# Random-feature attention with four heads side by side, one ring of banks, and the first cross-attention queries made a stage earlier

## What is computed

```python
# L0_attn, per head h: q, k, v are 112 x 16; omega is 16 x 64
qf = exp(q @ omega - 0.5 * sum(q*q))       # 112 x 64
kf = exp(k @ omega - 0.5 * sum(k*k))       # 112 x 64
kv  = kf.T @ v                             # 64 x 16, the sums
z   = kf.sum(0)                            # 64
out = (qf @ kv) / (qf @ z + 1e-6)          # numerator / denominator
x = layernorm(x + concat(out) @ Wout + bout)
# L0_xattn: q = x @ Wq + bq, keys and values from the text, softmax over 375
```

## Time and profile before

| | us |
|---|---|
| median of 3 runs (lowest to highest) | 1277.84 (1275.55 to 1280.85) |
| time of the profiled execution | 1264.48 |
| its span, first to last instruction | 1262.6 |
| granted TensorE clock over the span | 0.901 |
| PE busy | 1054.4 (84%) |
| DVE / ACT / POOL busy | 663.6 / 581.2 / 281.5 |

### The profile page before, as it was taken

The page is one execution under the profiler, slowest core; times in us unless marked ns, Lnnn a source line. Parts: engine busy times, 40 slices in busy tenths (PEclk is TensorE's granted clock), DMA queues, the critical chain, the costliest instruction groups (busy, mean ns, idle before and its releaser), DMA issues.

```text
span 1262.6 us, 20956 instructions
## 1 busy us (share of the span) xinstructions
PE 1054.4 (84%) x8288; PEld 758.4 (60%) x8288; DVE 663.6 (53%) x1646; ACT 581.2 (46%) x1368; POOL 281.5 (22%) x285
## 2 busy tenths in 40 slices
PE   7988678888784777788999878888988888778996
PEld 4677446566444777545556566666766666445654
DVE  3322455556673767345445547776676774535103
ACT  5411237545334555344444525555565564455542
POOL 2410213200150000332112110222212222232543
PEclk9876759879886999898999999999999998768998
DMA  9420225410455683354224304431332105000001
GB/s 321 92 44 1 55 64 123 129 28 11 165 175 201 217 324 123 115 164 148 85 71 139 120 33 152 125 99 34 90 98 75 50 1 208 1 1 1 1 1 30
DMA packets 66593, 123.63 MB, mean 98 GB/s; under 512 B 11536, under 2 KB 42224, under 8 KB 62416
## 3 DMA queue, kind: packets, MB, share of 16 engines
q1 hardware_dynamic: 63728, 117.48, 30.4%
q0 software_dynamic: 1536, 3.67, 0.9%
q10 hardware_dynamic: 1232, 1.15, 0.3%
HBM read 86.30 MB, written 35.92 MB: 97 GB/s over the span
## 4 chain that ended last, share of the span: by engine, by line
PE 56%; DVE 19%; ACT 10%; DMA 5%; POOL 4%; SPq 3%; issue 3%; DVEq 0%; ACTq 0%; POOLq 0%
PE psum L385 39%; ACT s_p L2469 2%; DVE s_p L2511 2%; POOL rs L2801 2%; PE psum L1205 2%; DMA values<-s_v 2%; DVE s_max L2500 2%; PE psum L2428 2%; PE psum L2439 2%; PE psum L1177 1%; PE psum L2600 1%; DVE s_pT L2492 1%; SPq L960 1%; DVE s_max L1330 1%; DVE wu L1150 1%
## 5 line engine op out<-in xcount | busy, mean ns | idle before, releaser
L2469 ACT ACTIVATE s_p<-psum,s_max 112x375 f32<-112x375 f32 x128 | 72.3, 569 | 85.9 <-DVE s_max L2500 85.9
L633 POOL TENSOR_TENSOR rstd<-meanvar,minus_half 112x1 f32<-112x1 f32 x40 | 23.3, 584 | 315.1 <-DVE meanvar L608 271.2
L1330 DVE TENSOR_REDUCE s_max<-psum 112x2 f32<-112x750 f32 x64 | 59.4, 935 | 39.3 <-PE psum L1177 38.5
L2801 POOL TENSOR_TENSOR rs<-ms,minus_half 112x32 f32<-112x32 f32 x8 | 43.5, 5442 | 110.2 <-DVE ms L2735 110.2
L385 PE MATMUL psum<-ctx,Wk 128*128 128x375 f16 x320 | 62.3, 330 | 5.0 <-ACT s_yT L2058 2.8
L385 PE MATMUL psum<-Wv,ctx 128*125 128x512 f16 x240 | 59.7, 410 | 8.0 <-issue 2.7
L2500 DVE TENSOR_REDUCE s_max<-psum 112x1 f32<-112x375 f32 x128 | 63.7, 539 | 2.1 <-PE psum L2420 2.1
L2428 PE MATMUL psum<-ident,s_p 112*125 112x112 f32 x384 | 59.6, 288 | 4.7 <-DVE s_p L2511 3.0
L1274 ACT ACTIVATE s_pT<-psum 125x672 f32<-125x672 f32 x64 | 46.7, 731 | 32.2 <-PE psum L1193 30.6
L3111 POOL TENSOR_TENSOR hidden<-raw,hidden 128x448 f16<-128x448 f32 x44 | 45.7, 1038 | 65.3 <-ACT hidden L2994 63.6
L587 ACT ACTIVATE s_v<-psum 125x512 f32<-125x512 f32 x48 | 28.5, 596 | 67.3 <-PE psum L385 47.8
(11 more groups left out here) (353 smaller groups left out, 2570.0 us busy)
## 6 DMA issues: line engine op xcount, KB each, us to landing
keys<-s_k SPq DMA_DIRECT2D x64, 187.5 KB, 2.2
s_k<-keys SPq DMA_DIRECT2D x8, 1500.0 KB, 7.4
values<-s_v SPq DMA_DIRECT2D x48, 224.0 KB
s_v<-values SPq DMA_DIRECT2D x16, 672.0 KB
raw_wg<-in_wg SPq DMA_DIRECT2D x8, 1024.0 KB, 5.8
raw_wu<-in_wu SPq DMA_DIRECT2D x8, 1024.0 KB, 5.7
raw_wd<-in_wd SPq DMA_DIRECT2D x8, 1024.0 KB, 5.3
s_kd<-k_halves SPq DMA_DIRECT2D x48, 93.8 KB, 3.9
```

Of the source, the lines that this page charges most:

```text
L1330: VE.tensor_reduce(s1_max[b % 2][:, 2 * p:2 * p + 2], rings["s1"][unit][0:N, :, 0:S], X, ALU.max, negate=True).then_inc(*V.up("max1", n))
L2469: SC.activation(rings["p4"][2 * n + j], rings["s4"][(n, j)][0:N, 0:S], ACT.Exp, bias=s4_max[b % 2][:, h:h + 1], accum_out=s4_sum[b % 2][:, ...
L2801: GP.tensor_tensor(rs5[b % 2][:], ms5[b % 2][:], minus_half[:], ALU.pow).then_inc(*G.up("rs5", b))
```

## The change

1. **Sums** (`kvT0`, `kvT0e`, `kv0`, `kv0e`). For each batch 16 matmuls with 32 columns of `v_one` (now 32 a head, 16 of them ones) as weights and the 64 feature columns of the head moving, four heads in four strips of output partitions. ACT copies the result (128 x 256), two transposes turn it, DVE copies it once.
2. **Numerators** (`num0`, `num0e`, `turn0`, `turn0e`). 16 matmuls with 32 columns of `kv` as weights (64 rows) and 112 columns of `q_feat` moving, heads of even and odd number in a bank each; two ACT copies; four transposes; then the same three DVE operations as before. The order of heads that results is put into the rows of `Wout0`.
3. **Banks and streams.** All 8 banks are one ring, ordered by planned release; each batch is a stream of its own, with rests of 750 between its steps; evacuations are units of their own (`...e`). `v_one`, `kvT`, `kv` and `oT0` have 4 buffers each, in room that stage 0 did not use.
4. **First queries.** `q1`, `qput` and `qget` of batches 0 and 1 run in stage 0, once both are normalised and the last query feature has been made. `s1_q16` and `s1_qd` lie where `q_f` was. The other three pairs stay in stage 1.
5. **Loads.** x and `Wqkv` are loaded in two parts each, and the first projections wait for the first parts only. SP issues two DMAs more.

The diff, cut to its core (the code of `q1`, `qput` and `qget` moves unchanged but for the ring and a wait for the last feature; `kf0` and `v0` now wait for `kvT0` where they waited for `num0`, and the `...e` units for their buffers' last readers):

```diff
+    g_x1, g_wv0 = Group("dma_x1"), Group("dma_wv0")
+    every = slice(None)
+    g_x.fill_part("xT", x_ch, every, every, slice(0, HALF))
     g_x.fill("chan", chan)
-    Wqkv = g_w0.load(wts, "Wqkv", [P, KC, 3 * D])
+    g_x1.fill_part("xT", x_ch, every, every, slice(HALF, T_))
+    Wqkv = wts.tensor("Wqkv", [P, KC, 3 * D])
+    g_w0.fill_part("Wqkv", Wqkv, every, every, slice(0, 2 * D))
     omega = g_w0.load(wts, "omega", [P, 4 * FM])
-    vbias0 = g_w0.load(wts, "vbias0", [N, D])
+    g_wv0.fill_part("Wqkv", Wqkv, every, every, slice(2 * D, 3 * D))
+    vbias0 = g_wv0.load(wts, "vbias0", [N, D])
...
+    end0, _ = work.at, work.restart(later)
+    s1_q16 = [work.tensor(f"s1_q16_{i}", [P, KC, 2, 2 * N], F16) for i in range(2)]
+    s1_qd = [work.tensor(f"s1_qd{i}", [P, HP, 2, N], F16) for i in range(2)]
+    after_queries, _ = work.at, work.restart(end0)
...
-    v_one = [work.tensor(f"v_one{i}", [N, H, DH + 1]) for i in range(2)]
-    kv = [work.tensor(f"kv{i}", [P, H // 2, 2 * (DH + 1)]) for i in range(2)]
+    spare = Region(nc, ringm.base, 24 * KB)
+    v_one = [spare.tensor(f"v_one{i}", [N, H, 2 * DH]) for i in range(4)]
+    kvT = [spare.tensor(f"kvT{i}", [P, 4 * FM]) for i in range(4)]
+    kv = [spare.tensor(f"kv{i}", [P, 2, P]) for i in range(4)]
+    oT0 = [spare.tensor(f"oT0_{i}", [P, 2, 2, N]) for i in range(4)]
...
-    W34 = 2 * (DH + 1)
-    rings["proj0"], rings["misc0"] = banks(0, 4), banks(4, 4)
+    rings["misc0"] = rings["q1r0"] = banks(0, 8, by_release=True)
     step("start", "V +3, V ones0, G zeros, G +1, G ident16, G identh, G +2, G ones1")
     step("zero")
-    step("qk0", "T proj0, V qk0a, A qk0a, V qk0b, A qk0b", "proj0", "V qk0b, A qk0b", 1500)
-    step("feat0", "T feat0, A feat0", "proj0", "A feat0", 750)
+    step("q1", "T q1, A q1, V q1", "q1r#", "V q1", 750)
+    step("qput")
+    step("qget")
+    step("kvT0", "T kvT0", "misc0", "A kvT0", 600)
+    step("kvT0e", "A kvT0")
+    step("kv0", "T kv0", "misc0", "V kv0", 400)
+    step("kv0e", "V kv0")
+    step("num0", "T num0", "misc0", "A num0", 350)
+    step("num0e", "A num0")
+    step("turn0", "T turn0", "misc0", "V att0", 700)
+    step("turn0e", "V +2, V att0")
...
+    def head0(g, j):
+
+        return 8 * (g // 2) + 2 * j + g % 2
...
     def s0_batch(b):
         yield from until(("feat0", b // 4, H // 2 - 1))
+        if b >= 2:
+            yield from until(("kvT0", b - 2))
         for t0 in (0, 2):
             yield [("kf0", b, t0)]
         yield [("v0", b), ("bias", 0, b)]
+        yield from rest(REST / 2)
+        yield from until_free("misc0", 3)
+        yield [("kvT0", b)]
+        yield from rest(REST / 2)
+        if b >= 4:
+            yield from until(("kv0", b - 4))
+        yield [("kvT0e", b)]
+        yield from rest(REST / 2)
+        yield from until_free("misc0", 3)
         yield [("kv0", b)]
-        yield from rest(REST)
-        yield [("num0", b)]
-        yield from rest(REST)
+        yield from rest(REST / 2)
+        if b >= 4:
+            yield from until(("num0", b - 4, 1))
+        yield [("kv0e", b)]
+        yield from rest(REST / 2)
+        yield from until_free("misc0", 4)
+        yield [("num0", b, 0), ("num0", b, 1)]
+        yield from rest(REST / 2)
+        if b >= 4:
+            yield from until(("turn0", b - 4))
+        yield [("num0e", b, 0), ("num0e", b, 1)]
+        yield from rest(REST / 2)
+        yield from until_free("misc0", 3)
+        yield [("turn0", b)]
+        yield from rest(REST / 2)
+        if b >= 2:
+            yield from until(("attT0", b - 2))
+        yield [("turn0e", b)]
+        yield from rest(REST / 2)
+        yield from until_free("misc0", 3)
         yield [("attT0", b)]
         yield from rest(REST / 2)
+        if b >= 2:
+            yield from until(("out", 0, b - 2))
         yield [("attT0e", b)]
-        yield from rest(REST)
+        yield from rest(REST / 2)
         yield [("out", 0, b)]
-        yield from norm_and_turn(0, b)
+        yield from norm_and_turn(0, b, free=3)
...
+    def s1_queries(b):
+        for c in range(KC):
+            yield [("q1", b, c)]
+        yield [("qput", b)]
+        if b >= 4:
+            yield from until(("st1", (b - 2) * HP - 1))
+        yield [("qget", b)]
+
+    def s0_queries():
+        yield from until(("xTe", 0, 0), ("xTe", 0, 1), ("feat0", 1, H // 2 - 1))
+        yield from s1_queries(0)
+
     place(("start",))
     for i in range(SLOTS // HC):
         L_zero.plan(("zero", i))
     place(("zero",))
     for i in range(3):
         place_ctx(i)
-    weave(follow(s0_features, (0, 1)), follow(s0_batch, range(0, B, 2)),
-          follow(s0_batch, range(1, B, 2)), s0_keys())
+    weave(follow(s0_features, (0, 1)), *(s0_batch(b) for b in range(B)),
+          s0_keys(), s0_queries())
...
+            elif what == "kvT0":
+                b, = at
+                ring = rings["misc0"]
+                pe.wait_ge(A["kf0", b, 2], V["v0", b], *ring.free(unit))
+                for g in range(4):
+                    for j in range(4):
+                        h = head0(g, j)
+                        ins = TE.matmul(ring[unit][32 * j:32 * j + 32, g * FM:(g + 1) * FM],
+                                        v_one[b % 4][:, h, :],
+                                        k_feat[b % 2][:, h * FM:(h + 1) * FM], start=True, stop=True)
+                ins.then_inc(*T.up("kvT0", b))
             elif what == "kv0":
                 b, = at
-                i, ring = b % 2, rings["misc0"]
-                pe.wait_ge(A["kf0", b, 2], V["v0", b], *ring.free(unit))
-                for pair in range(H // 2):
-                    mm(ring[unit][:, pair * W34:(pair + 1) * W34],
-                       [(k_feat[i][:, pair * P:(pair + 1) * P],
-                         v_one[i][:, 2 * pair:2 * pair + 2, :].rearrange("p h d -> p (h d)"))],
-                       T.up("kv0", b) if pair == H // 2 - 1 else None)
+                ring = rings["misc0"]
+                pe.wait_ge(A["kvT0", b], g_const.ready, *ring.free(unit))
+                for c in range(2):
+                    ins = TE.transpose(ring[unit][:, c * P:(c + 1) * P],
+                                       kvT[b % 4][:, c * P:(c + 1) * P], ident[:])
+                ins.then_inc(*T.up("kv0", b))
             elif what == "num0":
+                b, odd = at
+                hf, lc = b // 4, slice(b % 4 * N, (b % 4 + 1) * N)
+                ring, rows = rings["misc0"], slice(64 * odd, 64 * odd + 64)
+                pe.wait_ge(V["kv0", b], A["feat0", hf, H // 2 - 1], *ring.free(unit))
+                for c in range(2):
+                    for j in range(4):
+                        ins = TE.matmul(ring[unit][32 * j:32 * j + 32, c * N:(c + 1) * N],
+                                        kv[b % 4][rows, c, 32 * j:32 * j + 32],
+                                        q_feat[hf][rows, head0(2 * c + odd, j) // 2, lc],
+                                        start=True, stop=True)
+                ins.then_inc(*T.up("num0", b, odd))
+            elif what == "turn0":
                 b, = at
-                i, hf, lc = b % 2, b // 4, slice(b % 4 * N, (b % 4 + 1) * N)
                 ring = rings["misc0"]
-                pe.wait_ge(V["kv0", b], A["feat0", hf, H // 2 - 1], *ring.free(unit))
-                for pair in range(H // 2):
-                    mm(ring[unit][0:N, pair * W34:(pair + 1) * W34],
-                       [(q_feat[hf][:, pair, lc], kv[i][:, pair, :])],
-                       T.up("num0", b) if pair == H // 2 - 1 else None)
+                pe.wait_ge(A["num0", b, 1], *ring.free(unit))
+                for odd in range(2):
+                    for c in range(2):
+                        at_ = (2 * odd + c) * P
+                        ins = TE.transpose(ring[unit][0:N, at_:at_ + P], oT0[b % 4][:, odd, c, :],
+                                           ident[:])
+                ins.then_inc(*T.up("turn0", b))
...
+            elif what == "kvT0e":
+                b, = at
+                if b >= 4:
+                    act.wait_ge(T["kv0", b - 4])
+                act.wait_ge(T["kvT0", b])
+                SC.activation(kvT[b % 4][:], rings["misc0"][("kvT0", b)][:, 0:4 * FM],
+                              ACT.Copy).then_inc(*A.up("kvT0", b))
+            elif what == "num0e":
+                b, odd = at
+                if b >= 4:
+                    act.wait_ge(T["turn0", b - 4])
+                act.wait_ge(T["num0", b, odd])
+                SC.activation(oT0[b % 4][:, odd],
+                              rings["misc0"][("num0", b, odd)][:, 0:2 * N].rearrange(
+                                  "p (c n) -> p c n", n=N), ACT.Copy).then_inc(*A.up("num0", b, odd))
...
-            elif what == "kv0":
+            elif what == "kv0e":
                 b, = at
+                if b >= 4:
+                    dve.wait_ge(T["num0", b - 4, 1])
                 dve.wait_ge(T["kv0", b])
```

(34 more changed lines are left out.)

125 lines of the change are left out of this document (58 added, 67 removed).

## The result

The changed kernel took 1239.77 us (median of 4 runs, 1233.76 to 1247.93) where that of before took 1276.69 us: a ratio of 0.9715, with a 95% interval of 0.9669 to 0.976. Forecast were 1236 us and a range of 1215 to 1258. Its profiled execution took 1241.81 us with a span of 1240.0 us.

A forecast was written before the change was run, and what follows sets the result against it. PE was taken to bound stage 0. Stage 0 would lose 29.2 us and the start of stage 1 13, together 42.2: the profiled 1264.5 becomes 1222, plus 13.4 to the median gives 1236 us, range 1215 to 1258.

The forecast's parts named there:

- the sum for stage 0: Stage 0: PE work of 86.9 us at clock 0.96, start and idle time added, ends at 105.0 instead of 134.2 us.
- the prediction's own last sign: Start of stage 1: the forecast falls if the first transposed score comes more than 25 us after stage 0 ends.
- Products: Stage 0 sums and numerators on PE: 2.49 us a batch with transposes instead of 3.29, 6.4 us less for eight.
- The drain: Stage 0 on PE: by the skill's rule, 32 tiling mode switches would cost 5.4 us more, making the time 1241.
- Clock: PE's granted clock in stage 0: taken as 0.96, bounds 0.71 and 1.00.
- Idle time: PE in stage 0: 8.5 us idle, 3.4 for the last batch's bare end and 5.1 for the lengthened chain.
- Start: First matmul of stage 0: waits for fewer bytes, so starts at 6.0 us, 2.4 us earlier; bounds 0 and 2.7.
- Boundary: Stage 0's end to first transposed score: 17.9 instead of 32.9 us; 13 us less after 2 slip into the loop.
- the low clock: Rival, stage 0 on PE: the clock stays at 0.71 after 53 us, total 1250; chance 0.17.
- the bias: Rival, stage 0: DVE stands at the first output addition waiting for the bias, PE runs dry, total 1244; chance 0.10.
- the serial strips: Rival, stage 0 products: strips don't run beside each other, 7.7 us a batch, total 1297, slower; chance 0.03.
- The rival that the loop takes the early start back: Rival, stage 1 main loop: only 5 instead of 13 us gained at the boundary, total 1244; chance 0.12.

The follow-up runs named there:

- DVE was freed: Changed kernel with batch 3's keys placed behind the sending of batch 0's maxima, and s1_v's two memsets on POOL instead of DVE: 1230.96 us, ratio 0.9632 to before.

## Why the prediction was right, point by point

The whole was forecast as 42.2 us less and came as 34 to 37. The direction and the sum for stage 0 held by their mechanism; that the whole landed within 4 us of 1236 is in part luck. Stage 0 gave 2 to 7 us more than its 29.2, and the boundary about 10 us less than its 15. By the prediction's own last sign, a first transposed score more than 25 us late, the forecast falls: it came 28.3 and 28.4 us after the boundary in the two traces.

- **Products:** I took 2.49 us a batch, it is 1.86. The sums I priced at 0.8 by the count of matmuls cost 0.52, close to the bound by columns. The numerators cost 0.61 instead of 0.95. The direction and the source of the price held; the size was off by 5 us in my favour, which hid part of the miss at the boundary.
- **The drain** of the Trainium skill (TensorEngine Tiling, Key Properties) would have added 5.4 us. The trace does not show it: after the sums the next matmul starts at 34.58 us, before their recorded end at 34.65, and all four parts together, taken from start to start so that a drain between them would be inside, cost less than I had taken without it. (Recorded ends are modelled, so the second weighs more.) The whole can't decide: 1239.77 us lies between 1236 and the 1241 with the drain.
- **Clock:** I took 0.96. It was 1.00 up to 50 us and 0.92 behind that, 0.96 in the second trace of the changed kernel. That the 34-column products are a cause was only argued from the earlier trace rows; with them back in the new streams the clock was 0.79, against 0.90 to 0.97 in the eight traces with new products and new streams. What in these products lowers it stays open.
- **Idle time:** 8.5 us forecast, 9.2 measured. The lengthened chain is covered, but by the eight streams only.
- **Start:** 6.0 us forecast, 7.8 measured. The step that failed is "at 308 GB/s that is 2.7 us". It priced the bytes and left out the issue and the slower stretch of 4 to 7 us. Asking for 0.82 MB less won 0.6 us (8.41 to 7.79); asking for 0.37 MB less in whole arrays won 1.3 (8.41 to 7.08). The second trace of before starts at 10.23 us, so the start of before itself scatters by more than this.
- **End of stage 0:** 105.0 forecast, 102.8 and 100.6 measured.
- **Boundary:** this is the step that failed: "17.9 us instead of 32.9". It counted DVE's maxima and took it that PE's work would "nearly fit". 28.3 and 28.4 us were measured. I had summed PE's work in the gap and not read its order, in which the keys of batch 3 stand before the sixth score; nor had I followed where SP issues the context they need. Before the change this wait lay inside the queries' round trip. With the keys later it is 21.4 us, so this wait is 6.9 of the missing 10.4 us. The other 3.5 us are PE's as far as the traces tell, for when DVE was freed only 1 us changed. The sum held "12 us" of PE's work at full clock against 17.9 us of time; at the 0.74 of this stretch 12 us take 16, and PE was busy for 17.94 us in it.
- **Loop:** I let 2 us slip into it. Both kernels' loops take 133 to 138 us and overlap; no slip shows.
- **Whole:** 29.2 + 13 forecast; by the traces 31.4 and 36.2 in stage 0 and 36.8 to 39.7 up to the end of stage 1.

Of the rivals, the low clock (0.92 and 0.96 behind 50 us), the bias (the first four additions end on POOL by 53.7 us, the first output addition on DVE starts at 73.6) and the serial strips did not occur. The rival that the loop takes the early start back named the right size (4 to 5 us are left at the boundary) and the right place with the wrong mechanism: the start itself came late.

## What to carry to other kernels

Before taking a round trip out of a gap, read the order of the bound engine through the whole gap and ask of each instruction in it what it waits for; the wait that comes next can leave 5 us of a gain that was reckoned as 15. Reckon that engine's work at the clock which the stretch has. Splitting a product into shorter steps with more hand-overs pays in full only together with enough independent streams to cover them: here the products alone gave 5 us, the streams with their ring 16, both 32 to 34. And compare at an event in the middle of the kernel, since untouched later stages scatter by more than many a change is worth.

## What the runs showed that I had not expected

- With loads in parts the first four issues took 0.57 to 0.70 us each instead of 0.41 to 0.43, the whole arrays among them too, and from 4 to 7 us the DMA engines moved 173 to 249 GB/s instead of 363 to 418. The half of x alone moved at 374.
- Sixteen fp32 matmuls with 64 rows and 112 columns, in four strips, take 0.61 us; twelve with 125 rows and as many columns take 0.71 us. The order of strips mattered for the sums (112 rows, four in a row in one strip: 1.03 to 2.33 us for two batches) and hardly for the numerators (64 rows, two in a row: 1.23 to 1.32 us); rows and run length changed together. Whether the two halves of the rows run at once was not tried by itself.
- Under the same streams PE had a granted clock of 0.79 with 34-column products and was busy 61.2 of 69.0 us; with the new products it had 0.92 at 43.6 of 52.8 us. The share of recorded busy time was the higher one where the clock was the lower. With the new products in the other strip order it was 0.97 at 48.0 of 56.0 us: there more busy time came with more clock, so the busy share does not put these three in order.
